# Routed language-model tower on one core: column arithmetic, group sums, weight copies and idle products rearranged

## Time and profile before

| | us |
|---|---|
| median of 3 runs (lowest, highest) | 186.21 (184.81, 190.72) |
| span of the profiled execution | 157.3 |
| its own time | not given apart; the median less the span is 28.9 |
| TensorE busy | 122.2 (78%) |
| VectorE busy | 114.8 (73%) |
| GpSimd busy | 93.0 (59%) |
| ScalarE busy | 73.4 (47%) |

### The profile page before, as it was taken

The page is one execution under the profiler, slowest core; times in us unless marked ns, Lnnn a source line. Parts: engine busy times, 40 slices in busy tenths (PEclk is TensorE's granted clock), DMA queues, the critical chain, the costliest instruction groups (busy, mean ns, idle before and its releaser), DMA issues.

```text
span 157.3 us, 3532 instructions
## 1 busy us (share of the span) xinstructions
PE 122.2 (78%) x807; PEld 96.5 (61%) x807; DVE 114.8 (73%) x480; ACT 73.4 (47%) x236; POOL 93.0 (59%) x114
## 2 busy tenths in 40 slices
PE   0067896938989968876996899999999999999300
PEld 0022355516837736743894689999999999983000
DVE  0899965899598999878647767587777778734573
ACT  3040882028167106038444356777877777760000
POOL 4778779300077677527756777777777776674000
PEclk9999699997559998589599999999999999997555
DMA  4411111991027271125315412444333111110896
GB/s 118 112 50 36 50 50 46 201 276 52 0 44 230 67 231 60 52 68 108 80 38 133 104 53 69 129 114 116 102 84 94 40 37 50 48 36 0 269 331 201
DMA packets 15093, 15.65 MB, mean 99 GB/s; under 512 B 2995, under 2 KB 11701, under 8 KB 15074
## 3 DMA queue, kind: packets, MB, share of 16 engines
q1 hardware_dynamic: 11058, 9.43, 23.6%
q0 software_dynamic: 2784, 5.28, 10.6%
q10 hardware_dynamic: 1232, 0.72, 1.5%
HBM read 9.62 MB, written 6.27 MB: 101 GB/s over the span
## 4 chain that ended last, share of the span: by engine, by line
PE 23%; issue 9%; DVE 6%; POOL 6%; DMA 5%; DVEq 1%; SPq 1%; ACT 1%; POOLq 0%; ACTq 0%
PE bank L1195 7%; PE bank L1181 7%; PE bank L1171 6%; POOL results L367 6%; DMA yres<-results 3%; DVE act_h L727 1%; PE bank L1161 1%; DMA results<-ysb,dest 1%; SPq L280 1%; DVEq L713 1%; DVE res L820 1%; PE bank L1051 1%; DVE res L824 1%; ACT rows L872 0%; DVE arg L609 0%
## 5 line engine op out<-in xcount | busy, mean ns | idle before, releaser
L356 POOL DMA_INDIRECT sorted_rows<-rows,slot x32 | 32.2, 1007 | 29.1 <-DVE slot L629 20.0
L716 DVE COPY w1b<-w_sb 128x516 f32 x39 | 18.9, 486 | 13.5 <-DVE act_h L727 5.7
L727 DVE SCALAR_TENSOR_TENSOR act_h<-bank,w1b,sil 128x128 f32<-128x128 f32 x78 | 23.6, 343 | 4.8 <-PE bank L1181 1.6
L367 POOL DMA_INDIRECT results<-ysb,dest x22 | 21.6, 983 | 7.9 <-issue 7.3
L1195 PE MATMUL bank<-w_sb,act_h 128*128 x156 | 25.1, 285 | 1.0 <-issue 0.5
L1181 PE MATMUL bank<-xT,w1b 128*128 128x128 f32 x156 | 24.6, 281 | 1.5 <-DVE act_h L727 1.4
L928 ACT ACTIVATE sil<-bank,w1b 128x128 f32<-128x128 f32 x78 | 24.4, 364 | 0.3 <-PE bank L1171 0.2
L1171 PE MATMUL bank<-xT,w1b 128*128 128x128 f32 x156 | 24.4, 280 | 0.0
L1181 PEld LDWEIGHTS bank<-xT,w1b 128*128 128x128 f32 x156 | 21.0, 195 | 2.1 <-DVE act_h L727 2.1
L1195 PEld LDWEIGHTS bank<-w_sb,act_h 128*128 128x128 f32 x156 | 20.9, 195 | 2.0 <-issue 1.9
L367 POOL DMA_INDIRECT results<-ysb,xt x17 | 16.8, 990 | 7.2 <-issue 3.7
(11 more groups left out here) (236 smaller groups left out, 189.7 us busy)
## 6 DMA issues: line engine op xcount, KB each, us to landing
w_sb<-w_all SPq DMA_DIRECT2D x8, 386.0 KB, 5.8
xt<-sorted_rows SPq DMA_DIRECT2D x39, 65.0 KB, 2.0
yres<-results SPq DMA_DIRECT2D x8, 256.0 KB, 4.9
sorted_rows<-pad SPq DMA_DIRECT2D x1, 520.0 KB, 6.6
sorted_rows<-rows,slot POOLq DMA_INDIRECT x32, 2.7
out<-res SPq DMA_DIRECT2D x2, 256.0 KB, 3.9
results<-ysb,dest POOLq DMA_INDIRECT x22
results<-ysb,xt POOLq DMA_INDIRECT x17
```

Of the source, the lines that this page charges most:

```text
L356: gp.indirect_dma_start(sorted_rows[:, :], bass.IndirectOffsetOnAxis(ap=slot[:, k, t:t + 1], axis=0), rows[:, k, t, :], None).then_inc(s_s ...
L367: gp.indirect_dma_start(results[:, :], bass.IndirectOffsetOnAxis(ap=target, axis=0), ysb[i][:, :], None, bounds_check=bound, oob_is_err=Fa ...
L716: v.tensor_copy(w1b[i % 4][:, :], w_sb[:, bass.ds(at, W1)]).then_inc(s_wb, 1)
L727: v.scalar_tensor_tensor(act_h[i % 2][:, q], ps_l[sides(i)][:, q], w1b[i % 4][:, 2 * HID + 2 + c:2 * HID + 3 + c], sil[i % 2][:, q], ALU.a ...
```

## The change

- `prm` is loaded from ScalarE's queue, ahead of the positions, and no longer from SP's.
- The column arithmetic is one interleaved list: radius, 1/Lambda and the parts of B_bar that need no cosine are steps between those of the angle. `embed_and_radius` becomes `embed_and_inputs`, without them. `decay` stands before `normed_u(0)`.
- GpSimd issues all 16 gathers in a row and adds positions to group 3 alone. VectorE adds group 2 itself, after scan 0 (`embed(2, GT)`); the statistics of group 3 are taken after `choose(0)`. `norm("x0", "u2", "u3")` becomes `norm("x0", "u2")`, and `norm("x1")` becomes `norm("x1", "u3")`.
- ScalarE copies the weights of tiles 0 to 8, with the nine addresses loaded in `first_list`: copy 0 before `gelu(3)`, 1 and 2 after it, 3 in tile 0 before `normed_x(3)`, 4 to 8 in tiles 1 to 5 before `keep`. VectorE copies from tile 9 on. `copied(i)` names the semaphore.
- TensorE has twelve more idle products in group 2's turn: three after `turn_u(2)`, six after `skipped(2)`, three after `logits(1)`; `turn_u(3)` stands between the halves of `rotated(2)`.

The diff, cut to its core (the removed lines of the two column functions are in the code printed above; of the interleaved list its helpers and two stretches stand for the rest):

```diff
-NORMS = ["u0", "u1", "x0", "u2", "u3", "x1", "x2", "x3"]
-NORM_DONE = {"u0": 2, "u1": 4, "x0": 6, "u2": 6, "u3": 6, "x1": 8, "x2": 10, "x3": 12}
+NORMS = ["u0", "u1", "x0", "u2", "x1", "u3", "x2", "x3"]
+NORM_DONE = {"u0": 2, "u1": 4, "x0": 6, "u2": 6, "x1": 8, "u3": 8, "x2": 10, "x3": 12}
...
+        def copied(i):
+            return (s_wa, i + 1) if i < FULL[0] else (s_wb, i - FULL[0] + 1)
...
-            sp.dma_start(prm[:, :], prm_in).then_inc(s_prm, 16)
...
-            gather(0)
-            gather(1)
+            for g in range(NG):
+                gather(g)
...
-            gather(2)
-            gather(3)
...
-            for g in (2, 3):
-                pool.wait_ge(s_gath[g], 16 * GT)
-                e = res[:, GT * g:GT * g + GT, :]
-                gp.tensor_tensor(e, e, pos_sb[:, :, :], ALU.add).then_inc(s_emb, 1)
+            pool.wait_ge(s_gath[NG - 1], 16 * GT)
+            e = res[:, GT * (NG - 1):NT, :]
+            gp.tensor_tensor(e, e, pos_sb[:, :, :], ALU.add).then_inc(s_emb, 1)
...
+            def nearest(dst, src):
...
+            def unshifted(dst):
...
+            x = nearest(C(NN), LS)
+            i = begin(v.tensor_tensor(C(DEN), LR, LR, ALU.mult))
+            until(x)
+            x = unshifted(C(NN))
+            until(i)
+            i = begin(v.scalar_tensor_tensor(C(DEN), LI, LI, C(DEN), ALU.mult, ALU.add))
+            until(x)
+            x = less(C(FF), C(NN), -LN2_HI, LS)
+            power(C(PW), C(NN))
...
+            until(x)
+            x = begin(v.tensor_scalar(C(HI), C(HI), HI_MAGIC, None, ALU.subtract))
+            until(r)
...
+            def embed(g, at=0):
...
+                    begin(v.bn_stats(stats[:, at + j, :], res[:, GT * g + j, :]))
+                settle()
...
+            def embedded_sums(g, at):
+                dve.wait_ge(s_emb, 1)
...
+                    begin(v.bn_stats(stats[:, at + j, :], res[:, GT * g + j, :]))
...
+            def embed_and_inputs():
...
+                    return begin(v.bn_stats(stats[:, j, :], res[:, j, :]))
...
+                dve.wait_ge(s_trig, 2)
+                begin(v.tensor_scalar(C(NRE), cosw[:, 1:2], C(RM), -1.0, ALU.mult, ALU.add))
+                x = begin(v.tensor_tensor(C(NIM), sinw[:, 1:2], C(RM), ALU.mult))
...
+                begin(v.tensor_tensor(C(T0), C(NIM), C(Q1), ALU.mult))
+                x = begin(v.tensor_tensor(C(T1), C(NIM), C(P1), ALU.mult))
...
+                begin(v.scalar_tensor_tensor(C(CA), C(NRE), C(P1), C(T0), ALU.mult, ALU.add))
+                x = begin(v.scalar_tensor_tensor(C(CB), C(NRE), C(Q1), C(T1), ALU.mult, ALU.subtract))
...
+                    begin(v.bn_aggr(st[:, j, :], stats[:, j, :]))
+                settle()
...
+                dve.wait_ge(s_bc, 32)
+                begin(v.tensor_scalar(btmp[:, 0, :], bm[:, 1, :], C(CB), None, ALU.mult))
...
+                x = begin(v.tensor_scalar(btmp[:, 1, :], bm[:, 0, :], C(CB), None, ALU.mult))
...
+                step(v.tensor_tensor(w, a, var, ALU.mult))
+                dve.wait_ge(s_rooth, 1)
+                step(v.tensor_scalar(root_h[:, 0:GT, 1:NR], w[:, :, None].to_broadcast([P, GT, NR - 1]), -1.0, None, ALU.add))
+                step(v.tensor_tensor_scan(root_p[:, 0:GT, :].rearrange("p j k -> p (j k)"),
+                                          root_h[:, 0:GT, :].rearrange("p j k -> p (j k)"), series[:, 0:GT * NR], 0.0,
+                                          ALU.mult, ALU.add))
...
             def expert_weights(i):
...
-                if i >= 4:
-                    dve.wait_ge(s_a, 2 * i - 6)
+                dve.wait_ge(s_a, 2 * i - 6)
...
             def gated(i):
...
-                        dve.wait_ge(s_wb, i + 1)
+                        dve.wait_ge(*copied(i))
...
-            dve.wait_ge(s_rooth, 1)
-            embed_and_radius()
+            embed_and_inputs()
...
             norm("u1")
             scan(0)
-            embedded_sums(2)
-            embedded_sums(3)
+            embed(2, GT)
             add_gelu(0)
-            norm("x0", "u2", "u3")
+            norm("x0", "u2")
             scan(1)
             choose(0)
+            embedded_sums(3, GT)
             find_slots(0)
             add_gelu(1)
-            norm("x1")
+            norm("x1", "u3")
             scan(2)
             choose(1)
             find_slots(1)
...
             scan(3)
...
             choose(2)
-            dve.wait_ge(s_table, 2)
-            dve.wait_ge(s_w, 16 * NE)
-            expert_weights(0)
-            expert_weights(1)
             find_slots(2)
...
             add_gelu(3)
             norm("x3")
...
-                if i + 2 < NTILES:
+                if FULL[0] <= i + 2 < NTILES:
...
+            act.dma_start(prm[:, :], prm_in).then_inc(s_prm, 16)
...
+            act.wait_ge(s_radius, 1)
+            a.activation(decay[:, :].rearrange("p (b t) -> p b t", b=2),
+                         ktab[:, None, 0:SEQ].to_broadcast([P, 2, SEQ]), ACT.Identity,
+                         bias=col[:, 31:32], scale=0.0).then_inc(s_decay, 1)
+            act.wait_ge(s_decay, 1)
+            a.activation(decay[:, SEQ:SEQ + 1], ktab[:, 0:1], ACT.Identity, scale=0.0).then_inc(s_decay, 1)
...
+            def first_list():
+                act.wait_ge(s_table, 2)
+                act.wait_ge(s_w, 16 * NE)
+                return nc.values_load_multi_w_load_instructions(
+                    tile_wi[0:1, 0:FULL[0]], engines=[mybir.EngineType.Activation], min_val=0, max_val=(NE - 1) * WE,
+                    skip_runtime_bounds_check_because="starts of an expert's weights, made from the expert's number")[1]
...
+            def copy_weights(i):
+                if i >= 4:
+                    act.wait_ge(s_a, 2 * i - 6)
+                a.copy(w1b[i % 4][:, :], w_sb[:, bass.ds(starts[i], W1)]).then_inc(s_wa, 1)
...
-            act.wait_ge(s_radius, 1)
-            a.activation(decay[:, :].rearrange("p (b t) -> p b t", b=2),
-                         ktab[:, None, 0:SEQ].to_broadcast([P, 2, SEQ]), ACT.Identity,
-                         bias=col[:, 31:32], scale=0.0).then_inc(s_decay, 1)
-            act.wait_ge(s_decay, 1)
-            a.activation(decay[:, SEQ:SEQ + 1], ktab[:, 0:1], ACT.Identity, scale=0.0).then_inc(s_decay, 1)
...
-            normed_u(3)
...
-            copy_uT(3)
+            normed_u(3); copy_uT(3)
...
+            starts = first_list()
+            copy_weights(0)
             gelu(3)
+            copy_weights(1)
+            copy_weights(2)
...
             def gate(i):
...
-                act.wait_ge(s_wb, i + 1)
+                act.wait_ge(*copied(i))
...
                 if i == 0:
+                    copy_weights(3)
...
+                if 1 <= i and i + 3 < FULL[0]:
+                    copy_weights(i + 3)
...
             turn_u(2)
+            idle_products(3, ps_xT[1])
             b_times_u(2)
             skipped(2)
+            idle_products(6, ps_xT[1])
             turn_x(1)
+            logits(1)
+            idle_products(3, ps_xT[1])
+            rotated(2, 0)
             turn_u(3)
-            logits(1)
-            rotated(2, 0)
...
             def first(i):
-                pe.wait_ge(s_wb, i + 1)
+                pe.wait_ge(*copied(i))
...
```

More of the change, by code:

```diff
@@ new lines, in less, with taylor_sum @@
+            def less(dst, n_, part, src):
+                return begin(v.scalar_tensor_tensor(dst, n_, part, src, ALU.mult, ALU.add))
+            def taylor_sum(row, f):
+                return begin(v.tensor_tensor_scan(horner[:, row, :], f.to_broadcast([P, NH]), taylor, EXP_TAYLOR[0],
+                                                  ALU.mult, ALU.add))
+            dve.wait_ge(s_prm, 16)
+            x = nearest(C(NN), LS)
+            i = begin(v.tensor_tensor(C(DEN), LR, LR, ALU.mult))
@@ new lines, in _ @@
+            until(x)
+            x = begin(v.tensor_scalar(C(KT), C(TH), 1 / (2 * PI), MAGIC, ALU.mult, ALU.add))
+            until(r)
+            r = nearest(C(NR_), C(T1))
+            until(x)
+            x = begin(v.tensor_scalar(C(KT), C(KT), MAGIC, None, ALU.subtract))
+            until(r)
+            r = unshifted(C(NR_))
+            until(x)
+            x = begin(v.scalar_tensor_tensor(C(TH), C(KT), -TWO_PI_1, C(TH), ALU.mult, ALU.add))
+            until(r)
+            r = less(C(FR), C(NR_), -LN2_HI, C(T1))
@@ new lines, in _ @@
+            until(x)
+            x = begin(v.scalar_tensor_tensor(C(TH), C(KT), -TWO_PI_2, C(TH), ALU.mult, ALU.add))
+            until(r)
+            r = less(C(FR), C(NR_), -LN2_LO, C(FR))
+            until(x)
+            x = begin(v.scalar_tensor_tensor(C(TH), C(KT), -TWO_PI_3, C(TH), ALU.mult, ALU.add))
+            power(C(PR), C(NR_))
+            until(x)
+            x = begin(v.tensor_scalar(C(TU), C(TH), 1 / (2 * PI), None, ALU.mult))
+            until(r)
+            r = taylor_sum(1, C(FR))
```

130 lines of the change are left out of this document (45 added, 85 removed).

## The result

The changed kernel took 190.47 us in the median of four runs (189.74 to 191.56), the kernel before beside it 187.98 (184.81 to 190.72): ratio 1.0286, 95% interval 1.0202 to 1.0369, **slower**, where 180.1 and faster had been forecast. The ratio leaves out executions more than 1.5% above a kernel's fastest: of the kernel before that leaves 184.81 and 186.21, so it is larger than the 1.013 between the medians. The span of the execution profiled is 189.8 us, and the other three span 188.0 to 188.8, each 1.7 to 1.9 us less than its time.

What follows compares the result with a forecast made beforehand. GpSimd's back-to-back scatters from result 2 were taken to set the end, so gains counted up to result 1 (-4.8); scatter 2 -5.0 and the last scatter -6.1 gave 186.21 - 6.1 = 180.1 us, range 177 to 185.

Steps and rivals of the forecast that it cites:

- 28.9 us lie around the span, if the profiled run is an average one: Whole kernel before: profiled span 157.3 us, median time 186.21; the 28.9 us between were taken to lie outside the span.
- Beginning (-2.0): Start up to scan 0: prm loaded first on ScalarE's queue and interleaved column steps start scan 0 at 18.7, 2.0 us sooner.
- Group two's sums (-4.65): After scan 0: VectorE adds group two itself instead of waiting for GpSimd; GELU add at 25.1, 4.65 us sooner.
- clock in groups one and two (-5.9): TensorE after scan 1: full clock kept because the empty stretch nearly vanishes; group one's GELU add at 36.9, 5.9 us sooner.
- rival B: Group one: the clock falls after all, rotated(1) takes 1.7 us longer; +1.3 us, 181.4 in all; chance 0.13.
- Idle products in group two (0): TensorE, group two: twelve added idle products hidden under waits at full clock, costing nothing; 2.8 us if those waits are gone.
- Rival E: Group two: half clock lasts, idle products fall on the path, the end comes 4 us later, 190.2, slower; chance 0.06.
- Nine addresses (2.7, hidden): ScalarE before copy 0: nine address loads at the median price, 2.7 us in all, finished without delaying the path.
- rival C: ScalarE's nine addresses cost 0.55 us each: +1.9 us, 182.0 in all; chance 0.08.
- The stage of x3 (-5.5 to -4.8): From x3's rows to result 1: rows at 67.9, 5.5 us sooner; result 1 scattered at 78.4, 4.8 sooner.
- rival A: Stage of x3: full clock there too for products ahead of choose(3), 2.2 us sooner, 177.9 in all; chance 0.17.
- Rival D: Little gained: late gathers or ScalarE's copies leave result 1 only 2 to 3.5 us sooner; 182.7 to 185; chance 0.16.

Runs made afterwards that it cites:

- b_fourth: The kernel before, run again unchanged on chip D, where every trace has stops (engines standing together, no known releaser): 191.26 us, ratio 0.9951.
- b_third: The kernel before, run again unchanged on chip B, where traces show no such stops: 157.84 us.
- a_third: The changed kernel, run again unchanged on chip B: 153.40 us, ratio 0.9716 to the kernel before.
- a_fourth: The changed kernel, run again unchanged on chip D, where traces have stops: 190.94 us, medians 0.997 of the kernel before.
- a_again: The changed kernel, run again unchanged on chip A, without stops: 154.62 us, ratio 0.9724 to the kernel before.
- e_gsplit: The changed kernel with the gathers of groups two and three back behind GpSimd's constants, chip A: 153.66 us, ratio 0.9729 to the kernel before.
- m_fill: The changed kernel with seven instead of two idle products in tile 0 before turn_last_x, chip C: 152.85 us, ratio 0.9608 to the kernel before.

## Why the prediction was wrong

**The step that failed** is the first: "28.9 us lie around the span, if the profiled run is an average one". It was not. 1.7 to 1.8 us lie around a span of the kernel before, wherever span and time are known of the same execution, so 157.3 belongs to a time near 159, and the median of 186.21 to another regime, in which some 27 us more of standing lie inside the span. The sum was made on a timeline that the timed executions did not have. In b_fourth the stops and the slower loop add 33.0 us up to the last scatter: 7.6 by scan 0, 6.1 from there to result 1, 6.3 to result 10, and 13.0 in the loop behind it.

On the timeline that it was made for, the sum fared well: a span of 151.2, where spans of the changed kernel were 149.4 to 153.7 on chips A and B. That is in part luck, since more was gained up to x3's rows than forecast and some of it lost behind them. Times of the stages (us), without stops (chip B) and with (chip D):

| | forecast | b_third | a_third | b_fourth | a_fourth |
|---|---|---|---|---|---|
| embedding add, group one | 14.6 | 15.9 | 14.4 | 19.6 | 15.4 |
| scan 0 | 18.7 | 20.8 | 18.0 | 28.4 | 28.2 |
| GELU add, group zero | 25.1 | 28.9 | 24.3 | 36.4 | 35.4 |
| scan 1 | 29.1 | 33.3 | 28.5 | 40.8 | 39.4 |
| GELU add, group one | 36.9 | 41.7 | 36.1 | 49.2 | 47.8 |
| slots of group one | 48.2 | 51.9 | 47.3 | 61.8 | 60.5 |
| x3's rows | 67.9 | 71.6 | 66.8 | 81.9 | 81.2 |
| choose(3) | 74.5 | 77.4 | 74.3 | 90.8 | 89.4 |
| result 1 | 78.4 | 80.6 | 79.3 | 94.3 | 94.0 |
| result 2 | 90.1 | 92.6 | 90.8 | 106.0 | 105.5 |
| result 10 | | 102.9 | 101.1 | 122.9 | 123.9 |
| last scatter | 136.6 | 140.3 | 137.6 | 173.3 | 174.9 |

The rows of a_third behind its column, VectorE then GpSimd:

```profile
14.40 0.71 DVE L533 TENSOR_TENSOR res<-res,pos_sb 128x512 f32<-128x512 f32 x1 [0.32 <-DMA res<-emb_table,tok_sb]
18.01 0.68 DVE L606 TENSOR_TENSOR rot<-bank,cosw 128x512 f32<-128x512 f32 x1
24.31 0.46 DVE L625 TENSOR_TENSOR res<-res,gel 128x256 f32<-128x256 f32 x1
...
74.32 0.39 DVE L634 MAX8 top<-bank 128x8 f32<-128x8 f32 x4 [2.78 <-PE bank L1093]
...
79.26 0.99 POOL L366 DMA_INDIRECT results<-ysb,xt  x1 [2.31 <-ACT ysb L987]
137.60 0.98 POOL L366 DMA_INDIRECT results<-ysb,dest  x1 [0.30 <-issue]
```

**Beginning (-2.0).** Without stops right: scan 0 at 18.0, -2.8 on chip B. With stops the same work is done sooner and then held, with scan 0 4 to 5 us behind the last gather: -0.15. Whether the order of the gathers decides it was not tried on such a chip.

**Group two's sums (-4.65), clock in groups one and two (-5.9).** Right without stops: GELU adds at 24.3 and 36.1 in a_third, with the full clock from 24 to 54 us. In a_again the clock was 0.50 from 34 to 36 us (rival B) and the second add came at 37.3, 0.4 after the forecast. With stops -1.0 and -1.4.

**Idle products in group two (0).** Right: with and without, 153.40 and 153.62. Rival E is refuted without stops, and with them TensorE was no slower there by the stage times (slots of group one at 60.5 for 61.8).

**Nine addresses (2.7, hidden).** Mis-sized: all nine came by one instruction of 0.97 us, a third of the price, as the forecast's argument against rival C had it. ScalarE stood 4.0 us ahead of copy 0 in a_again, but 2.9 of them for the list, which VectorE finished at 59.58. It stayed hidden, as said. The Trainium skill ("DMA: Bandwidth & Descriptors", "Latency and other measured facts") gives a `tensor_load` a floor of about 600 ns; the single loads of a_again took 0.30 us in the median, and the nine together less than two such floors. VectorE's write of the list, ScalarE's load and its copy 0 in a_again:

```profile
59.43 0.15 DVE L696 CAST tile_wi<-bank 1x9 int32<-1x9 f32 x1
L926 ACTq TENSOR_LOAD <-tile_wi x1: 967/967/967, 59.6 to 59.6; - x1
60.69 0.62 ACT L933 COPY w1b<-w_sb 128x516 f32 x1 [4.00 <-issue]
```

**The stage of x3 (-5.5 to -4.8).** Without stops this is the mis-sized term, the ground of rivals A and D. It rested on the earlier trace rows of one execution, whose mean clock from x3's rows to `choose(3)` was 0.74; rival A took that stretch of 6.56 us for one at half clock and priced the full clock at 2.2 us. With a mean of 0.64 (a_third) it took 7.5 us, at 1.00 5.8 in the kernel before (b_third) and 5.2 in e_gsplit and m_fill. b_third was at result 1 2.6 us sooner (80.62) than the profiled execution; a_third had the half clock. So -4.8 at x3's rows became -3.1 at `choose(3)` and -1.4 at result 1. With the full clock in both (e_gsplit on chip A 77.47, b_third on chip B 80.62) it is -3.2. The clock in this stage differs between executions of one kernel, and the sum took it as fixed. Rival D's times don't follow from its own text: result 1 1.3 to 2.8 us later than forecast gives 181.4 to 182.9, not 182.7 to 185.

**"The floor of the end is the time of scatter 2".** Right without stops: scatters 2 to the last follow at 46.84 / 36 = 1.30 us in a_third, 0.8 us less in all than in b_third (1.15 had been forecast). With them GpSimd waits for `ysb` (22.7 us in b_fourth, 25.8 in a_fourth), and 173.26 - 105.97 = 67.3 us pass from result 2 to the last, where 47.7 did in b_third.

**Why slower.** On chips D and E no loss of 2.9% came back: 190.94 beside 191.26 and 191.44. In the traces of that chip the gain is gone, all but 0.3 us, by result 1, in stages with stops, and 1.4 us went between results 2 and 10 (from 0.5 sooner to 0.9 later), where ScalarE has copies 5 to 8 that VectorE had (0.62 each). That these are the cause with stops is argued, not shown. In the comparison the kernel before ran at 184.81, 186.21, 189.74 and 190.72 and the changed one at 189.74 to 191.56: the 2.9% rest on the two lower ones. Single executions as low came on the chips with stops too, of the changed kernel (183.67 on D) and of m_fill (187.56 on E). Why an execution is lower, and whether the change makes it rarer, stays open.

## What to carry to other kernels

Before making a sum on a profiled execution, hold its span against the timed runs: if more than a few us lie between, the profile shows another regime than the one timed, and the difference has to be explained first. Of this change, what is won without stops survives (2.8%), and with them nothing does. One trace does not give the clock of a stage: read it in several executions before a term rests on it, and before a variant is said to have changed it. And the idle time ahead of an instruction is not the price of what stands before it in the list: see first when its input was ready.
